# Router logits by four column strips turned back on TensorE, reciprocal roots on GpSimd, number pattern filled by three engines

## What is computed

```python
xn = _layernorm(x)                                    # (x - m) / sqrt(v + eps), per token
# recurrence branch
x_conv = causal_depthwise_conv(xn, 4 taps) + conv_b
r, i = sigmoid(x_conv @ W_r.T + b_r), sigmoid(x_conv @ W_i.T + b_i)
a = sigmoid(log_a) ** (8 * r)
h[t] = a[t] * h[t-1] + sqrt(clip(1 - a*a, 0)) * i * x_conv
o = h @ W_out.T;  attn = o * rsqrt(mean(o*o) + 1e-6) * gamma
# expert branch: 8 experts, room for 512 tokens each
probs = softmax(xn @ Wr);  e = argmax(probs)
rank = number of earlier tokens of the same expert;  keep = rank < 512
y = relu(xe @ W1[e]) @ W2[e] * probs[e]               # xe: the kept tokens of e, zero for the others
out = x + attn + y
```

## Time and profile before

| | before |
|---|---|
| median of 3 runs | 147.51 us (147.38 to 147.6) |
| span of the profiled execution | 128.8 us |
| median less span: what lies around the first and the last instruction | 18.7 us |
| PE, DVE, ACT, POOL busy | 106.2, 101.8, 99.6, 84.6 us |
| first gather starts, last scatter starts | 25.89, 111.35 us |
| transfers on POOL's queue from the first gather on | 64 |

### The profile page before, as it was taken

How to read it: one execution, slowest core, us unless ns; L and a number is a source line. 1 busy time by engine, 2 the same in 40 slices (tenths; PEclk the granted TensorE clock), 3 DMA queues, 4 the chain that set the end, 5 groups by cost and what they waited for, 6 DMA issues and landing times.

```text
span 128.8 us, 2229 instructions
## 1 busy us (share of the span) xinstructions
PE 106.2 (82%) x711; PEld 89.9 (70%) x711; DVE 101.8 (79%) x238; ACT 99.6 (77%) x219; POOL 84.6 (66%) x109
## 2 busy tenths in 40 slices
PE   3999999999799999999999997999997999700000
PEld 3999976672379779789879987898697899600000
DVE  5398998999699999979614489999999975973690
ACT  3299792888589589789689999999999799823560
POOL 8987774078788787778777877888787878700000
PEclk9999999999999999999999999999999999998555
DMA  2966964892456365312611711111110111149995
GB/s 85 383 247 173 405 244 173 318 380 66 103 169 181 80 209 139 118 53 56 209 41 41 219 51 41 61 37 41 52 57 25 60 43 61 41 108 302 325 372 215
DMA packets 8234, 19.27 MB, mean 150 GB/s; under 512 B 1689, under 2 KB 1945, under 8 KB 8224
## 3 DMA queue, kind: packets, MB, share of 16 engines
q1 hardware_dynamic: 5424, 13.70, 31.5%
q0 software_dynamic: 2080, 4.19, 11.2%
q10 hardware_dynamic: 720, 1.25, 2.6%
HBM read 10.82 MB, written 8.39 MB: 149 GB/s over the span
## 4 chain that ended last, share of the span: by engine, by line
PE 60%; DVE 9%; DMA 8%; ACT 8%; issue 5%; POOL 4%; POOLq 1%; SPq 1%; DVEq 0%; ACTq 0%
PE bank L624 17%; PE bank L609 6%; PE bank L611 6%; PE bank L610 6%; DMA dec<-y_rows 4%; PE bank L640 4%; PE bank L453 3%; PE bank L561 3%; PE bank L442 3%; POOL xn_tok L405 3%; DMA xn_tok<-xn_rows,idx_in 2%; ACT xc L796 2%; PE bank L594 2%; PE bank L563 2%; PE bank L562 2%
## 5 line engine op out<-in xcount | busy, mean ns | idle before, releaser
L405 POOL DMA_INDIRECT xn_tok<-xn_rows,idx_in x32 | 33.7, 1054 | 14.4 <-issue 9.4
L417 POOL DMA_INDIRECT y_rows<-xn_tok,idx_out x32 | 33.5, 1047 | 9.7 <-issue 9.1
L624 PE MATMUL bank<-w_raw,h_sb 128*128 128x128 f32 x256 | 29.9, 275 | 0.0
L624 PEld LDWEIGHTS bank<-w_raw,h_sb 128*128 128x128 f32 x256 | 29.2, 192 | 0.0
L786 ACT ACTIVATE h_sb<-bank 128x512 f32<-128x512 f32 x32 | 18.8, 598 | 2.5 <-PE bank L611 0.6
L609 PE MATMUL bank<-xg_hi,w_hi 128*128 128x512 f32 x32 | 13.2, 412 | 0.0
L611 PE MATMUL bank<-xg_hi,w_lo 128*128 128x512 f32 x32 | 12.6, 393 | 0.0
L610 PE MATMUL bank<-xg_lo,w_hi 128*128 128x512 f32 x32 | 12.5, 391 | 0.0
L1021 DVE SCALAR_TENSOR_TENSOR xc<-xnT,par,xc 128x1020 f32<-128x1020 f32 (+2 forms) x9 | 11.5, 1277 | 0.3
L640 PE MATMUL bank<-par,xc 128*128 128x128 f32 x64 | 8.8, 280 | 2.2 <-ACT xc L796 1.3
L1061 DVE TENSOR_TENSOR_SCAN xnT<-dec,bank 128x256 f32<-128x256 f32 x16 | 10.1, 674 | 0.3
(11 more groups left out here) (143 smaller groups left out, 243.2 us busy)
## 6 DMA issues: line engine op xcount, KB each, us to landing
w_raw<-in_weights SPq DMA_DIRECT2D x8, 512.0 KB, 3.9
y_rows<-sca SPq DMA_DIRECT2D x4, 512.0 KB, 5.9
dec<-y_rows SPq DMA_DIRECT2D x8, 256.0 KB, 5.7
x_tok<-in_x SPq DMA_DIRECT2D x3, 512.0 KB, 5.9
xn_rows<-xn_tok SPq DMA_DIRECT2D x3, 512.0 KB, 3.6
out<-dec SPq DMA_DIRECT2D x4, 256.0 KB, 3.1
out<-dec ACTq DMA_DIRECT2D x4, 256.0 KB, 2.9
x_tok<-in_x SPq DMA_DIRECT2D x2, 256.0 KB, 3.5
```

The lines of the kernel that those rows point to most:

```text
L405: g.indirect_dma_start(gathered[:, s * D:(s + 1) * D], None, xn_rows, bass.IndirectOffsetOnAxis(ap=idx_in[:, s:s + 1], axis=0)).then_inc(g ...
L417: g.indirect_dma_start(y_rows, bass.IndirectOffsetOnAxis(ap=idx_out[:, s:s + 1], axis=0), gathered[:, s * D:(s + 1) * D], None, bounds_che ...
L624: last = mm(tile_of(e, s), h_sb[:, k * CAP + s * P:k * CAP + (s + 1) * P], w_raw[:, e, F + k * D:F + (k + 1) * D], start=(k == 0), stop=(k ...
```

## The change

- **Router.** PE turns groups 0 to 5 of x first, then makes the logits of a half (four groups) with four matmuls: the router matrix, cut to 32 columns, is stationary in one of four column strips of the array, and 512 tokens move. The logits come out with experts in partitions; ACT copies them out (`keep_logits`) and PE turns them back with four transposes (`by_token`). Warm-up matmuls at the start go from 7 to 5.
- **Reciprocal roots.** POOL makes them out of the moments: two `tensor_scalar`, a `pow` with -0.5 and a product for each unit (`inverse`). ACT's `root` and DVE's `inverse` go. POOL normalises 20 tiles and ACT 12, and `diag` is made before the first unit.
- **Number pattern.** POOL writes one quarter of `values`, ACT two and DVE one, as copies of a row `count16` that POOL writes.
- **Order and banks.** The table is summed in bank 7, which also held the totals of each expert, so ACT copies the totals to SBUF (`totals`) and the first table matmul waits for it. The table's five parts are cut apart and lie between `columns_of(4)` to `columns_of(7)`. SP stores the zeros only after the gathers of expert 0 have landed.

```diff
@@ -94,7 +96,10 @@
         xg_lo = sb("xg_lo", [P, CAP], F32R)
         ident = sb("ident", [P, P])
         centre = sb("centre", [P, P])
-        w_router = sb("w_router", [P, P])
+        w_router = sb("w_router", [P, STRIP])
+        count16 = sb("count16", [P, P], F16)
+        root = sb("root", [P, LARGEST])
+        totals = sb("totals", [P, E])
...
@@ -152,15 +158,15 @@
...
-        centred = bank[7][:, 0:P]
+        centred = bank[7][:, 0:STRIP]
...
-        logits = [bank[6][:, 0:PT * E], bank[2][:, 0:PT * E]]
-        table = bank[3][:, 0:NS]
-        before = [bank[7][:, 0:E * PT], bank[6][:, 2 * E * PT:3 * E * PT]]
-        totals = bank[7][:, E * NT:E * NT + E]
+        strips = [bank[6], bank[2]]
+        table = bank[7][:, 0:NS]
+        before = [bank[3][:, 0:E * PT], bank[3][:, E * PT:2 * E * PT]]
+        counted = bank[7][:, E * NT:E * NT + E]
...
-        POOL_TILES = (2, 3, 6, 7, 10, 11, 14, 15, 18, 19, 22, 23, 26, 27, 30)
-        ACT_TILES = (0, 1, 4, 5, 8, 9, 12, 13, 16, 17, 20, 21, 24, 25, 28, 29, 31)
-
-        COUNT_AT = 6
+        ACT_TILES = (3, 7, 14, 15, 20, 21, 22, 23, 28, 29, 30, 31)
+        POOL_TILES = tuple(t for t in range(NT) if t not in ACT_TILES)
...
             sp.wait_ge(zeroed, 1)
+            sp.wait_ge(gather_in[0], 16 * ST)
             for c in range(C):
                 sp.dma_start(y_rows[c * TC:(c + 1) * TC, :].rearrange("(p j) d -> p (j d)", p=P),
                              zeros).then_inc(zero_out, 16)
...
+            g.memset(root[:, :], -0.5).then_inc(root_done, 1)
 
             pool.wait_ge(fill, 5)
             g.affine_select(out=ident16[:, :], in_=ident16[:, :], compare_op=ALU.not_equal, fill=1.0, base=0,
...
+            g.iota(values[:, 0:QUARTER, :], [[1, QUARTER], [0, NT]], base=0, channel_multiplier=0,
+                   **exact).then_inc(valued, 1)
+            pool.wait_ge(par_in, 16)
+            for k in range(TAPS):
+                if k == 0:
+                    pool.wait_ge(ident_done, 1)
+                g.tensor_scalar(diag[:, k, :], ident[:, :], par[:, CONV_W + k:CONV_W + k + 1], 0.0, ALU.mult,
+                                ALU.add).then_inc(diag_done, 1)
+
+            def inverse(u):
+                t0, nt = UNITS[u]
+                cols = slice(t0, t0 + nt)
+                pool.wait_ge(stat_done, (t0 + nt) // 2)
+                if u == 0:
+                    pool.wait_ge(root_done, 1)
+                g.tensor_scalar(std[:, cols], stats[:, cols, 2], 1.0 / D, LN_EPS, ALU.mult, ALU.add).then_inc(std_done, 1)
+                g.tensor_scalar(nmr[:, cols], stats[:, cols, 1], -1.0, None, ALU.mult).then_inc(minus_done, 1)
+                pool.wait_ge(std_done, u + 1)
+                g.tensor_tensor(rstd[:, cols], std[:, cols], root[:, 0:nt], ALU.pow).then_inc(rstd_done, 1)
+                pool.wait_ge(rstd_done, u + 1)
+                pool.wait_ge(minus_done, u + 1)
+                g.tensor_tensor(nmr[:, cols], nmr[:, cols], rstd[:, cols], ALU.mult).then_inc(nmr_done, 1)
+
             def normalise(u):
                 t0, nt = UNITS[u]
                 pool.wait_ge(nmr_done, u + 1)
...
-            def number(part):
-                v0, v1 = part * P // 4, (part + 1) * P // 4
-                g.iota(values[:, v0:v1, :], [[1, P // 4], [0, NT]], base=v0, channel_multiplier=0,
-                       **exact).then_inc(valued, 1)
-
-            for part in range(4):
-                number(part)
-            normalise(0)
-            normalise(1)
-            normalise(2)
-            pool.wait_ge(par_in, 16)
-            pool.wait_ge(ident_done, 1)
...
+            for u in range(NU):
+                inverse(u)
+                normalise(u)
...
             pe.wait_ge(ident_done, 1)
-            for _ in range(7):
+            for _ in range(5):
                 mm(bank[7][:, 0:P], ident[:, :], ident[:, :], start=True, stop=True)
...
+            def router(h):
+                if h == 0:
                     pe.wait_ge(router_w, 1)
-                transposed(pe, n)
-                for t in range(4 * n, 4 * n + 4):
-
-                    o = t % PT * E
-                    last = mm((bank[6], bank[2])[t // PT][:, o:o + D], xT[:, t * P:(t + 1) * P], w_router[:, :],
-                              start=True, stop=True)
+                transposed(pe, 4 * h + 3)
+                for j in range(P // STRIP):
+                    n = 4 * h + j
+                    last = mm(strips[h][j * STRIP:(j + 1) * STRIP, :], w_router[:, :], xT[:, n * HT:(n + 1) * HT],
+                              start=True, stop=True, tile_position=(0, j * STRIP))
+                last.then_inc(strips_done, 1)
+
+            def by_token(h):
+                pe.wait_ge(logitsT_done, h + 1)
+                for i in range(4):
+                    last = nc.tensor.transpose(strips[h][:, i * P:(i + 1) * P],
+                                               logitsT[h][:, i * P:(i + 1) * P], ident[:, :])
                 last.then_inc(logits_done, 1)
...
-            def table_of(h):
-                pe.wait_ge(hi_done, h + 1)
-                for t in range(h * PT, (h + 1) * PT):
-                    if t in LOW_STARTS:
-                        pe.wait_ge(low_done, LOW_STARTS.index(t) + 1)
-                    last = mm(table, low_eq[:, :, t], hi_val[:, h, :, :, t - h * PT].rearrange("p e s -> p (e s)"),
+            def table_of(t0):
+                t1 = (LOW_STARTS + (NT,))[LOW_STARTS.index(t0) + 1]
+                pe.wait_ge(hi_done, t0 // PT + 1)
+                pe.wait_ge(low_done, LOW_STARTS.index(t0) + 1)
+                if t0 == 0:
+                    pe.wait_ge(totals_done, 1)
+                for t in range(t0, t1):
+                    last = mm(table, low_eq[:, :, t],
+                              hi_val[:, t // PT, :, :, t % PT].rearrange("p e s -> p (e s)"),
                               start=(t == 0), stop=(t == NT - 1))
-                if h == NP - 1:
+                if t1 == NT:
                     last.then_inc(table_done, 1)
 
             def columns_of(n):
...
-                    counts(0)
+            turned(0)
+            pe.wait_ge(par_in, 16)
+            pe.wait_ge(centre_done, 1)
+            mm(centred, centre[:, :], par[:, ROUTER:ROUTER + STRIP], start=True, stop=True).then_inc(centre_mm, 1)
+            for n in range(1, 6):
+                turned(n)
+            router(0)
+            turned(6)
             columns_of(0)
-            router(NH - 1)
+            by_token(0)
+            turned(7)
+            columns_of(1)
+            router(1)
+            counts(0)
+            columns_of(2)
+            by_token(1)
+            columns_of(3)
 
             def conv(n, first, last_tap):
...
-                        pe.wait_ge(idx_done, 2)
+                        pe.wait_ge(lo_done, NP)
                 cols = slice(n * HT, (n + 1) * HT)
                 bnk = conv_bank[n % 2][:, :]
                 src = xnT[:, cols].rearrange("d (s l) -> d s l", l=L)
...
-                columns_of(n)
             conv(0, 0, 2)
             counts(1)
             for h in range(NP):
-                last = mm(totals, ones[:, :], run[:, h, :, PT - 1], start=(h == 0), stop=(h == NP - 1))
-            last.then_inc(before_done, 1)
+                last = mm(counted, ones[:, :], run[:, h, :, PT - 1], start=(h == 0), stop=(h == NP - 1))
+            last.then_inc(counted_done, 1)
+            conv(0, 2, 3)
             table_of(0)
-            columns_of(3)
-            conv(0, 2, 3)
-            table_of(1)
+            table_of(8)
+            columns_of(4)
             conv(0, 3, TAPS)
-            for n in range(4, NH):
-                columns_of(n)
+            columns_of(5)
+            table_of(16)
+            columns_of(6)
+            table_of(22)
+            columns_of(7)
+            table_of(28)
...
-            def root(u):
-                t0, nt = UNITS[u]
-                if u == 0:
-                    act.wait_ge(eps_done, 3)
-                act.wait_ge(stat_done, (t0 + nt) // 2)
-                a(std[:, t0:t0 + nt], stats[:, t0:t0 + nt, 2], ACT.Sqrt, bias=eps[:, 0:1],
-                  scale=1.0 / D).then_inc(std_done, 1)
...
+            def keep_logits(h):
+                act.wait_ge(strips_done, h + 1)
+                a(logitsT[h], strips[h][:, :], ACT.Copy).then_inc(logitsT_done, 1)
+
+            act.wait_ge(eps_done, 2)
+            act.wait_ge(count_done, 1)
+            for part in (1, 2):
+                v0, v1 = part * QUARTER, (part + 1) * QUARTER
+                a(values[:, v0:v1, :], count16[:, v0:v1].unsqueeze(2).to_broadcast([P, QUARTER, NT]),
+                  ACT.Copy).then_inc(valued, 1)
             untile(0)
             untile(1)
-            root(1)
+            untile(2)
+            untile(3)
+            untile(4)
             normalise(0)
-            untile(2)
             normalise(1)
-            root(2)
-            untile(3)
-            normalise(2)
-            untile(4)
```

(48 more changed lines are left out.)

94 lines of the change are left out of this document (43 added, 51 removed).

## The result

| | before | after |
|---|---|---|
| median | 147.56 us (147.38 to 148.07) | 158.69 us (157.91 to 160.53) |
| ratio | | 1.0715, 95% interval 1.0657 to 1.0772 |
| span of the profiled execution | 128.8 us | 156.2 us, of a run of 157.9 |
| first gather, last scatter start | 25.89, 111.35 us | 35.85, 139.03 us |

Ratios and their intervals leave out executions more than 1.5% above the fastest of their kernel; medians take in all.

A forecast was written before the change was run, and what follows sets the result against it. POOL's gapless queue from first gather to last scatter was taken to bound the kernel. Opening 0, totals behind the roots 1.1 and zeros 0 on 147.5 gave 148.6 us; likeliest range 147.9 to 149.8, stated range 147.1 to 151.5.

The forecast's parts named there:

- the term for `inverse`: POOL's reciprocal roots: 1.1 or 1.25 us per `inverse`, 5.95 for five, so the fifth `nmr` ends at 19.0.
- The rival of dear roots: POOL's roots: `pow` at 1.1 us makes five `inverse` 9.0, `idx_in` ends at 29.3, time 151.7 us; chance 0.13.
- The table's stretch: PE before `idx_in`: 32 table matmuls, four groups of columns and one convolution tap take 4.9 us.
- the clock as a rival: PE's opening: transposes don't engage the upper clock, time 150.7 us; chance 0.20 together with serial strips.
- Path one: Logits, ranks and table: second `run` near 18.3, table from 19.6, `idx_in` ends at 24.8, 0.3 us earlier than before.
- the rival of cheap roots: POOL's five `inverse` under 4.5 us: path one binds alone, `idx_in` ends at 24.8, time 147.2 us; chance 0.22.
- strips side by side: Router on PE: four strip matmuls overlap and take 0.9 us, against 3.4 one after another.
- the late zeros: SP's zero stores after gather 0, ending near 43.0: delay `decay(0)` 1.5 us, covered by 1.8 before scatter 0; priced 0.
- the pattern's quarters: Opening: quarters of `values`, near 1.1 us each on ACT and 0.75 on DVE, lie ahead of the first x; cost nothing.
- the link from the last tiles through the totals to the table: After the fifth `nmr`: ACT's four tiles 1.65, totals 0.2, hops 0.2; table begins at 21.05, `idx_in` 1.1 us later.
- One for one: Expert stage: POOL's queue has no slack, so the time moves by as much as the first gather's start.
- 18.7 us around the span: The median of 147.51 us was taken to lie 18.7 above the 128.8 us span with what is around it.

The follow-up runs named there:

- the old roots: Changed kernel with the roots back on ACT (square root) and DVE (reciprocal, product), zero stores still waiting: 152.92 us, no ratio.
- old roots and zeros early: Changed kernel with the roots back on ACT and DVE and the zeros stored without waiting for expert 0's gathers: 151.80 us, ratio 1.018.
- the lightened pair: Kernels before and after, each without two of three products of the expert's first layer: 148.06 and 158.91 us.
- `pow` twice: Changed kernel with each of POOL's five powers computed twice: 165.74 us, ratio 1.1047.
- the freed table: Changed kernel with ACT's totals copy ahead of its last four normalised tiles and table parts ahead of columns 5 to 7: 160.07 us, ratio 1.0512.
- before again: The kernel before, unchanged, run once more for a profile: 150.92 us, span 149.0 us.

## Why the prediction was wrong

- **The step that failed: the term for `inverse`.** I took 0.4 and 0.55 us for a `pow`, and 5.95 for the five `inverse`; they took 11.6. The `pow` is 1.04 for four columns and mostly 1.66 for eight, which as an estimate from two widths is 0.42 plus 0.155 a column; with a product in its place the same five are 5.4. Even my upper bound was no bound: I took the dearest row of POOL, 1.1, for a function of which no row existed. The rival of dear roots (9.0, 151.7 us) had the mechanism and stopped short of the size. Doubling, replacing and transplanting the `pow` each moved the first gather as this says; that is shown.
- **From there to `idx_in`.** The fifth `nmr` ended at 26.62 against 19.0: 5.7 of this from `inverse`, 0.4 from the start of the first, 0.8 from sixteen tiles at 0.48 in place of 0.435, some 0.8 from gaps between the groups. Behind it the chain over four tiles and totals took 1.9, as forecast (2.05).
- **The table's stretch**, 6.2 against 4.9: it is 5.0 at the upper clock, and here more than half of it ran at the lower one after PE's wait. I had the clock as a rival at the opening, not here. The two terms make 26.2 into 35.05.
- **Path one** was also short: the second `run` ended at 20.2 and 19.7 with the old roots and at 20.5 after, forecast 18.3. Part of it is the clock at the opening: it rose at 8.30 in after, at 5.34 in the trace of before, and the first strips started at 9.78, forecast 9.0; with old roots and zeros early it rose at 5.47 and they started at 9.11. That rival came true in part. In after PE turned the second logits back at 18.02, because `columns_of(2)` stands ahead of them and waited for POOL's tiles (ended 19.01 for the whole unit). It did not decide there; with cheap roots it would have (`idx_in` ended at 26.3 with old roots and zeros early, and at 28.7 with the product, forecast 24.8), so the rival of cheap roots was priced too low.
- **Right**: strips side by side, the late zeros and the pattern's quarters at nothing, the link from the last tiles through the totals to the table, the direction.
- **One for one**: shown for the lightened pair (10.85 us for 10.2). By ratios across chips, `pow` twice gave 5 us for 7.0 and the freed table 3 for 4.0, so somewhat less is possible in single cases.
- **18.7 us around the span**: wrong. In every run that lists both, the span lies 1.7 to 2.4 us below its time. The time of the trace shown is not on record, so that it was of a shorter execution of the same kernel is concluded, not measured. The bound that I read from it, a gapless POOL queue, does not hold in executions of the timed length: in before again POOL waits some 21 us for DVE's copies. Where it does, PE's results reach DVE late. The shift came out the same, since the kernels share this stage.
- **What stays open**: why PE's results reach ACT and DVE late in the expert stage, why PE pauses within a sum, and why the trace shown has neither. Less PE work doesn't remove it. That the late results come at a nearly fixed distance behind the first gather points at the gathers or at something they set off, but no run varied them. Another rival is the recording itself: the trace shown holds 2519 records of semaphores, the thirteen others 1526 to 1774, with most of the missing ones in the expert stage. Whether this and the pauses have one cause, no run shows; it also makes the releasers "issue" and "remote" weak evidence there. How the 3% that the product in place of `pow` leaves split between the clock, path one and chance is not settled either.

## What to carry to other kernels

A function that no row shows has no upper bound from other functions of its engine: before roots, powers or divisions move to GpSimd, measure one at the width that is used, and ask which single result of that queue an early table or a store hangs on. Before a sum is put on a median, compare the span of the trace with the time of its own run; if they are far apart, the trace shows another execution, and the bound read from it needs a second look. When a link to a slow chain is cut, look for the next link to the same chain: here the totals and the store both hung on the fifth `nmr`.

## What the runs showed of the hardware

- A `pow` of two tensors on GpSimd takes 1.04 us for 128x4 and 1.63 to 1.94 for 128x8, a product of the same shape 0.20, and so does an operation with one input. The Trainium skill (GPSIMD Engine Reference, Performance versus the Vector engine) has two-input elementwise work at about half of VectorE's rate; at these widths the rows don't show a difference of that kind (for 128x8 with two inputs, POOL's product 0.20, DVE's `nmr` in before 0.17), and the function decides.
- The granted clock rose at 8.30 in after. The last of ten records of warm-up products started at 4.11, the router's centring product ran from 5.40 to 5.88, and from 5.69 to 9.78 PE did transposes alone; they started 0.21 apart before the rise and 0.11 apart after it. In the other runs the clock rose between 5.3 and 8.3. The Trainium skill (TensorE: Matmul & The Clock Gate, Part 4) says that the upper clock "doesn't engage" for transposes; here it engaged in such a run, so the trace disagrees for transposes that follow products.
- Executions of the timed length hold two to five stretches of 3.4 to 10.2 us at half clock within the expert stage, in both kernels and their variants. In before again and in after, PE's idle times that are put down to issue reach 2.3 us there.
